# An adapter-plus-experts kernel: four buffers for x's parts, an own 98-row stack for the first tile's adapter product, a warm-up on a constant, folded parts ahead of bias sums

## What is computed

```python
y      = x @ W.T + b + 2.0 * (x @ lora_As[slot]) @ lora_Bs[slot]   # first layer, D = 512, R = 16
base   = y @ base_w.T + base_b                                     # second layer
hidden = y @ A.T                                                   # 128 x 64
probs  = softmax(y @ router_w.T)                                   # 128 x 16, two kept, divided by their sum
delta  = sum over experts e of  combine[e] * hidden @ B[e].T       # 1024 x 512 in all
out    = x + base + 0.5 * delta
```

## Time and profile before

| | us |
|---|---|
| median of three timed runs | 103.99 |
| lowest, highest | 103.49, 104.66 |
| the profiled execution: device time | 103.44 |
| the profiled execution: span of the profile | 101.6 |

### The profile page before, as it was taken

How to read it: one execution, slowest core, us unless ns; L and a number is a source line. 1 busy time by engine, 2 the same in 40 slices (tenths; PEclk the granted TensorE clock), 3 DMA queues, 4 the chain that set the end, 5 groups by cost and what they waited for, 6 DMA issues and landing times.

```text
span 101.6 us, 1806 instructions
## 1 busy us (share of the span) xinstructions
PE 97.4 (96%) x576; PEld 88.1 (87%) x576; DVE 65.1 (64%) x182; ACT 39.8 (39%) x97; POOL 18.7 (18%) x34
## 2 busy tenths in 40 slices
PE   5899999999999999999999999999999999999990
PEld 5799999999989999988988997899788788888990
DVE  2529999948567867959946735677368726656101
ACT  3404446885519726554435126120920604031000
POOL 5100003000397990070330061000000000000000
PEclk9999999999999999999999999999999999999999
DMA  2999789999854172592672280470065191940311
GB/s 42 321 318 377 225 182 372 340 424 422 230 96 68 26 216 58 168 267 68 182 254 59 79 231 1 117 205 6 14 165 165 20 266 46 239 170 0 110 52 52
DMA packets 8089, 16.91 MB, mean 166 GB/s; under 512 B 1475, under 2 KB 3907, under 8 KB 7952
## 3 DMA queue, kind: packets, MB, share of 16 engines
q1 hardware_dynamic: 7472, 16.40, 53.5%
q10 hardware_dynamic: 576, 0.39, 1.2%
q0 software_dynamic: 32, 0.00, 0.0%
HBM read 13.28 MB, written 2.16 MB: 152 GB/s over the span
## 4 chain that ended last, share of the span: by engine, by line
PE 71%; issue 11%; POOL 11%; DMA 3%; ACT 1%; DVE 0%; POOLq 0%
PE pair L771 69%; POOL x_lo L352 4%; POOL e_lo L370 4%; DMA w_raw_all<-w_cat 3%; POOL p_lo L364 2%; POOL p_hi L362 1%; PE pair L919 1%; PE pair L921 1%; ACT p_hi L418 1%; PE pair L939 1%; ACT w_hi_all L392 0%; DVE xn L765 0%; POOLq L361 0%
## 5 line engine op out<-in xcount | busy, mean ns | idle before, releaser
L771 PE MATMUL pair<-e_hi,w_hi_all 128*128 128x512 f32 (+1 forms) x72 | 27.2, 378 | 0.0
L771 PE MATMUL pair<-e_lo,w_hi_all 128*128 128x512 f32 (+1 forms) x72 | 26.7, 370 | 0.0
L771 PE MATMUL pair<-e_hi,w_lo_all 128*128 128x512 f32 (+1 forms) x72 | 26.6, 370 | 0.0
L771 PE MATMUL pair<-p_hi,x_hi 128*128 128x304 f32 x64 | 19.7, 308 | 0.2 <-POOL p_lo L364 0.2
L771 PE MATMUL pair<-p_lo,x_hi 128*128 128x304 f32 x64 | 19.4, 302 | 0.0
L771 PE MATMUL pair<-p_hi,x_lo 128*128 128x304 f32 x64 | 19.3, 302 | 0.0
L771 PEld LDWEIGHTS pair<-e_hi,w_lo_all 128*128 128x128 f32 x72 | 13.6, 188 | 2.6
L771 PEld LDWEIGHTS pair<-e_hi,w_hi_all 128*128 128x128 f32 x72 | 13.6, 188 | 2.4
L771 PEld LDWEIGHTS pair<-e_lo,w_hi_all 128*128 128x128 f32 x72 | 13.6, 189 | 1.8
L712 DVE TENSOR_TENSOR exp_raw_all<-w_raw_all 128x512 f32<-128x512 f32 x16 | 10.4, 689 | 7.5 <-DMA w_raw_all<-spill 7.5
L502 ACT ACTIVATE w_hi_all<-exp_raw_all 128x512 fp32r<-128x512 f32 x16 | 9.6, 627 | 13.8 <-DVE exp_raw_all L712 13.8
(11 more groups left out here) (107 smaller groups left out, 131.5 us busy)
## 6 DMA issues: line engine op xcount, KB each, us to landing
w_raw_all<-spill SPq DMA_DIRECT2D x16, 256.0 KB, 3.9
exp_raw_all<-experts SPq DMA_DIRECT2D x4, 512.0 KB, 8.7
xn<-x_n SPq DMA_DIRECT2D x4, 512.0 KB, 7.3
out<-xn SPq DMA_DIRECT2D x7, 256.0 KB, 4.0
w_raw_all<-w_cat SPq DMA_DIRECT2D x3, 552.0 KB, 6.8
xt_raw<-x_t SPq DMA_DIRECT2D x2, 512.0 KB, 6.3
xt_raw<-x_t SPq DMA_DIRECT2D x1, 1024.0 KB, 12.6
c_stack<-c_hi SPq DMA_DIRECT2D x7, 74.0 KB, 4.2
```

Source lines behind the costliest of these rows:

```text
L771: return nc.tensor.matmul(out_ap, lhs, rhs, start=first, stop=last)
```

## The change

1. **Warm-up.** It no longer reads `zeros` (F32R, set by DVE) but `nc.const_aps.tensor(0.0, (P, 2 * P), F32)`, a constant that the program's preamble sets, seen as 128x256; `WARM_UP` goes from 11 to 13; the wait for DVE is gone, and so is ACT's wait for the warm-up before `e_hi` is written.
2. **First tile.** `h_first` gets 2h rounded twice over (ACT, columns 0 to 15 and 64 to 79), the low part at column 32 (DVE), and ones at 96 and 97; its transpose, 98 rows, is copied once by ACT to `ht_first`; `c_first` (now `c_stack[:, 0]`) holds c high, c high again, c low and the bias rows at partitions 0, 32, 64 and 96, each copied there by ACT or DVE. The product is two matmuls. The bias rows of tiles 1 to 7 come by one DMA from it.
3. **x's parts** have four buffers (`XB`); those of tiles 2 and 3 lie in `w_hi` and `w_lo` of blocks 2 and 3, which are spent after the fold. ACT makes the high parts of tiles 2 and 3 right after the fold, POOL subtracts both before `lora_a_parts(2)`; for t >= 4 POOL does `lora_a_parts(t)` first.
4. **Bias sums.** `b1` and `b2` are issued behind the six tables; `b2` goes to row 0 of a zeroed 128x592 tensor, so the first bias sum is one instruction instead of two; the sums stand further back in DVE's order, behind the folded parts.
5. ACT splits the first half of W's first block in two pieces of 128 columns, and PE waits for each piece. `split_experts` stands elsewhere in ACT's order, and PE waits for POOL's expert parts only before the chunks that read them.

```diff
-WARM_UP = 11
+WARM_UP = 13
@@ tensors
-        b2_row = sb("b2_row", [1, D])
+        b2_rows = sb("b2_rows", [P, W2N])
-        zeros = e_hi[:, 0, 0:2 * P]
+        idle = nc.const_aps.tensor(0.0, (P, 2 * P), F32)
+        x_his, x_los = x_split(x_hi, w_hi), x_split(x_lo, w_lo)
@@ SP
-            sp.dma_start(b1_col[:, :], b1).then_inc(in_b, 16)
-            sp.dma_start(b2_row[:, :], b2).then_inc(in_b, 16)
             sp.dma_start(xt_raw[:, 0:2, :], x_t[:, 0:2, :]).then_inc(in_xt[0], 16)
...
+            sp.dma_start(b1_col[:, :], b1).then_inc(in_b, 16)
+            sp.wait_ge(first_set, 1)
+            sp.dma_start(b2_rows[0:1, SMALL:], b2).then_inc(in_b, 16)
@@ POOL
             x_lo_part(2)
+            x_lo_part(3)
             lora_a_parts(2)
             split_experts_lo(2)
-            x_lo_part(3)
             lora_a_parts(3)
             split_experts_lo(3)
             for t in range(4, NT):
+                lora_a_parts(t)
                 x_lo_part(t)
-                lora_a_parts(t)
@@ ACT
-            act.wait_ge(pe_warm, 1)
+            act.wait_ge(in_xt[1], 16)
+            x_hi_part(2)
+            x_hi_part(3)
             split_experts(0)
-            split_experts(1)
-            act.wait_ge(bias_step, KC + 1)
-            nc.scalar.activation(bp_hi[:, :], bias_part[:, :], ACT.Copy).then_inc(bph_done, 1)
             act.wait_ge(pe_c, 1)
             nc.scalar.activation(c_hi[:, :], w2_cols(ps_c), ACT.Copy).then_inc(ch_done, 1)
+            act.wait_ge(bias_step, KC)
+            nc.scalar.activation(bp_hi[:, :], bias_part[:, :], ACT.Copy).then_inc(bph_done, 1)
+            act.wait_ge(first_set, 2)
+            act.wait_ge(ch_done, 1)
+            nc.scalar.activation(c_first[0:R, :], c_hi[0:R, :], ACT.Copy).then_inc(first_high, 1)
@@ DVE
+            lora_first_lo()
+            dve.wait_ge(first_set, 2)
+            nc.vector.tensor_copy(c_first[F_AGAIN:F_AGAIN + R, :], c_hi[0:R, :]).then_inc(first_high, 1)
+            dve.wait_ge(cl_done, 1)
+            nc.vector.tensor_copy(c_first[F_LOW:F_LOW + R, :], c_lo[0:R, :]).then_inc(first_low, 1)
             split_experts_lo(0)
-            lora_first_lo()
             stack_bias()
@@ PE
-            pe.wait_ge(warm, 1)
             for _ in range(WARM_UP):
-                last = mm(ps_warm, zeros[:, 0:P], zeros, True, True)
-            last.then_inc(pe_warm, 1)
+                mm(ps_warm, idle[:, 0:P], idle, True, True)
...
@@ x_first
                 elif t == 1:
                     pe.wait_ge(cl_done, 1)
+                    pe.wait_ge(first_high, 2)
+                    pe.wait_ge(first_low, 1)
@@ lora_first_product
                 pe.wait_ge(ht_done, 1)
-                pe.wait_ge(ch_done, 1)
-                part(ht_first_hi[:, :], c_hi, False)
-                pe.wait_ge(cl_done, 1)
-                part(ht_first_hi[:, :], c_lo, False)
-                pe.wait_ge(ht_first_done, 1)
-                part(ht_first_lo[:, :], c_hi, False)
+                pe.wait_ge(first_high, 2)
+                pe.wait_ge(first_low, 1)
                 pe.wait_ge(bias_rows, 1)
-                part(ones[HR:HT, :], c_stack[HR:HT, 1, :], True).then_inc(pe_z, 1)
+                nc.tensor.matmul(ps_z[0][:, z_small[0]:BANK], ht_first[:, :], c_first[:, 0:border],
+                                 start=False, stop=True, skip_group_check=True)
+                nc.tensor.matmul(ps_z[0][:, BANK:BANK + W2N - border], ht_first[:, :], c_first[:, border:],
+                                 start=False, stop=True, skip_group_check=True).then_inc(pe_z, 1)
@@ lora_product
-                if t == 1:
-                    pe.wait_ge(bias_rows, 1)
-                else:
-                    pe.wait_ge(stacked_bias, 16)
+                pe.wait_ge(stacked_bias, 16)
```

More of the change, by code:

```diff
@@ L120, in adaln_ffn_kernel, with x_split @@
         rden = sb("rden", [P, 1])
+        def x_split(split, w_split):
+            return [split[:, b] for b in range(2)] + [
+                w_split[:, b, 0:D].rearrange("p (k n) -> p k n", k=KC) for b in range(2, XB)]
+        x_his, x_los = x_split(x_hi, w_hi), x_split(x_lo, w_lo)
         weight_rows = w_raw_all[:, 0:NB * GC * P].rearrange("p (a j n) -> p a j n", a=NB, j=GC)
@@ L391, in _ @@
             act.wait_ge(in_w_side[0], 16)
-            nc.scalar.activation(w_hi[:, 0, W_LEFT], w_raw[:, 0, W_LEFT], ACT.Copy).then_inc(wh_left, 1)
+            for cols in (slice(0, P), slice(P, 2 * P)):
+                nc.scalar.activation(w_hi[:, 0, cols], w_raw[:, 0, cols], ACT.Copy).then_inc(wh_left, 1)
             act.wait_ge(in_w_side[1], 16)
@@ L544, in _ @@
         def _(dve):
-            nc.vector.memset(zeros.bitcast(F32), 0.0).then_inc(warm, 1)
+            nc.vector.memset(b2_rows[:, :], 0.0).then_inc(first_set, 1)
+            nc.vector.memset(c_first.bitcast(F32), 0.0).then_inc(first_set, 1)
+            nc.vector.memset(h_first[:, :], 0.0).then_inc(first_set, 1)
             nc.vector.memset(ht[HR:HT, :, :].bitcast(F32), 1.0).then_inc(ht_set, 1)
             nc.vector.memset(routed[:, :, SMALL:T_H], 0.0).then_inc(ht_set, 1)
-            nc.vector.memset(low_row[HR:HT, :], -1.0).then_inc(low_row_set, 1)
-            dve.wait_ge(low_row_set, 1)
-            nc.vector.memset(low_row[HR:HR + 1, :], 0.0).then_inc(low_row_set, 1)
+            nc.vector.memset(low_row[F_BIAS:FT, :], -1.0).then_inc(first_set, 1)
+            dve.wait_ge(first_set, 4)
+            nc.vector.memset(h_first[:, F_BIAS:FT], 1.0).then_inc(first_set, 1)
+            nc.vector.memset(low_row[F_BIAS:F_BIAS + 1, :], 0.0).then_inc(first_set, 1)
             def first_block_hi(n, cols):
@@ L583, in x_lo_early @@
                 dve.wait_ge(xh_done, t + 1)
[L584 to L585 removed]
+                nc.vector.tensor_tensor(x_los[t], xt_raw[:, t, :].rearrange("p (k n) -> p k n", k=KC),
+                                        x_his[t].bitcast(F32),
                                         ALU.subtract).then_inc(xl_early, 1)
@@ L620, in _ @@
                                     ALU.subtract).then_inc(lbl_done, 1)
-            bias_part_of(0)
-            bias_part_of(1)
             folded_lo(0)
             folded_lo(1)
-            bias_part_of(2)
+            bias_part_of(1)
             folded_lo(2)
             folded_lo(3)
+            bias_part_of(2)
             bias_part_of(3)
+            dve.wait_ge(ch_done, 1)
+            nc.vector.tensor_tensor(c_lo[:, :], w2_cols(ps_c), c_hi[:, :].bitcast(F32),
+                                    ALU.subtract).then_inc(cl_done, 1)
             dve.wait_ge(bph_done, 1)
@@ L859, in x_side @@
                         pe.wait_ge(pl_done, KC)
-                    for n, (lhs, rhs) in enumerate(((x_hi, p_hi), (x_hi, p_lo), (x_lo, p_hi))):
-                        last = mm(ps_z[par][:, out_cols], lhs[:, par, k, :], rhs[:, k, cols],
+                    for n, (lhs, rhs) in enumerate(((x_h, p_hi), (x_h, p_lo), (x_l, p_hi))):
+                        last = mm(ps_z[par][:, out_cols], lhs[:, k, :], rhs[:, k, cols],
                                   k == 0 and n == 0, k == KC - 1 and n == 2)
```

130 lines of the change are left out of this document (61 added, 69 removed).

## The result

| | before | after |
|---|---|---|
| median of the timed runs, us | 103.72 (103.49 to 104.66) | 108.21 (107.29 to 108.60) |
| the profiled execution, us | 103.44 | 107.62 |
| its span, us | 101.6 | 105.7 |
| ratio after to before | | 1.040, 95% interval 1.033 to 1.047 |

Both medians are of five runs; the 103.99 further up is of the three that were there before the change.

The account below looks back on a forecast made before the run. TensorE's matmul stream was taken as the bound: its start, its length and a short tail. +4.26 - 1.0 - 0.25 = +3.0 us gave 106.4 on the profiled execution, 107.0 on the median; 106.7 was taken, range 104.8 to 109.0.

Parts of the forecast that it names:

- The warm-up, forecast at +4.26 us: Start of PE's stream: the fold begins 5.06 us later behind the longer warm-up, less 0.80 for faster first fold matmuls.
- everything behind it, forecast at -1.25: After the warm-up: 1.0 us saved at the first tile's product and 0.25 at the wait for POOL before `x_first(4)`.
- An F32 product is four passes: Warm-up: each F32 matmul takes four passes, 52 for 13 calls; with the clock rising within the warm-up, chance 0.80.
- The warm-up's end, 9.3 us: Warm-up on PE: 52 passes at 0.23 us until the clock rises at 5.5, then 0.12 each, end at 9.3.
- The slow matmuls come back: First six fold matmuls on PE: all run at the higher clock after the longer warm-up, giving back 0.80 us.
- The product, 1.0 us saved: First tile's product on PE: two matmuls replace eight and their holes, with PE about 0.1 us late for the bias rows.
- they are hidden with 0.4 to 0.5 us to spare: Before `x_first(1)`: ACT's and DVE's added copies ahead of the product end early enough that PE does not wait.
- POOL's chain, 0.25 saved: Before `x_first(4)`: POOL ends at 37.0 to 37.1, so PE's hole shrinks from 0.35 us to about 0.1.
- Bias sums: "Nothing": Later bias loads and DVE's sums: PE's margins for `lb_lo` and the folded parts suffice, so no time is lost.
- The one-pass rival: Warm-up: an F32 matmul costs one pass, the warm-up ends hidden at 3.9 us, total 102.6, 1.3% faster; chance 0.14.
- two passes for a call: Warm-up rival: 26 passes, end at 6.2 us, sum -0.1 us, total 103.9, no change; chance 0.04.
- the clock stay low to the end of the warm-up: Warm-up rival: four passes at the low clock throughout, end at 12.8 us, +7.3 us, total 111.3; chance 0.02.

Follow-up runs that it names:

- e1: The changed kernel with the warm-up's constant read as F32R instead of F32, still 13 matmuls: 104.73 us, ratio to before 1.006.
- e2: The kernel before with only the change's warm-up (13 F32 matmuls, no DVE memset, no ACT wait for the warm-up): 106.73 us, ratio to before 1.028.
- e4: The changed kernel with four F32 warm-up matmuls instead of 13: 104.75 us, ratio to before 1.008.
- e8: e1 with DVE's bias sums put back in the order of the kernel before: 103.61 us, ratio to before 0.997.
- e5: e1 with POOL waiting for DVE's last bias sum before x's low parts of tiles 2 and 3: 104.50 us, ratio to before 1.004.
- e7: e1 with the edits of both e5 and e6: 104.50 us, ratio to before 1.005.
- e6: e1 with DVE's subtraction of expert block 1 moved behind the routing of tile 1: 104.24 us, ratio to before 1.002.
- e9: e8 with expert block 1's subtraction given to POOL and ACT splitting expert block 2 before reading tile 1's h: 103.14 us, ratio to before 0.991.
- e10: e9 with tile 4's row copies issued behind the first routing trip instead of ahead of it: 103.50 us, ratio to before 0.991.

## Why the prediction was right, and where it was not

The forecast was slower, 106.7 us in a range of 104.8 to 109.0; measured 108.21, and 107.62 for the profiled execution against 106.4 forecast for it. The mechanism that carried it held. Two parts of the sum were off. The warm-up, forecast at +4.26 us, measured +3.35; everything behind it, forecast at -1.25, measured +0.75. The errors of -0.91 and +2.00 partly cancelled; that the number came out as near as it did is in part luck.

1. **An F32 product is four passes: right.** A call in the warm-up is two records, with starts 0.427 us apart at the lower clock and 0.218 at the higher; an F32R call of the same columns is one record, and the starts are 0.213 us apart at the lower clock (e1). So each of the two records costs two passes. e2 and e4 price it from both sides. The Trainium skill, "FP8 and Floating Point Precision", section "TensorE Precision Notes", gives four passes for true FP32; the trace agrees, with 2 x 0.427 us for a call against 0.213 for a pass.
2. **The warm-up's end, 9.3 us: too late by 1.0.** A pass cost 0.214 and 0.109, the columns alone, where I took 0.23 (an average with the first matmul's longer distance in it) and 0.12 (a stream that changes weights each time); and the clock rose 4.0 us after the first matmul instead of 4.7. The fold began at 8.27; the bound that I had worked out for columns only was 8.7. Net +3.35 instead of +4.26. The upper bound of this term, +5.4, is also 0.1 above what its own parts give (9.3 + 1.0 - 4.24 - 0.80 = 5.26).
3. **The slow matmuls come back: +0.80, measured 0.64.** Right in kind, and nearly in size: the first pair behind the warm-up took 0.46 only because the last warm-up record's 0.22 us fall into it. Items 2 and 3 share that overlap.
4. **The product, 1.0 us saved: the size of the work was right, the holes were not.** From the last matmul of `x_first(1)` to `x_other(1)` it takes 31.96 - 31.11 = 0.85 us instead of 1.51, which is 0.66 saved; the chain of the bias rows made a hole of 0.36 and not 0.1. The step "they are hidden with 0.4 to 0.5 us to spare" failed, with a hole of 0.28 us twice, as two bias sums took 3.11 us instead of 1.70 and `bp_hi`, which waits for them, stands ahead of h in ACT's order.
5. **POOL's chain, 0.25 saved: wrong.** The hole before `x_first(4)` went entirely, but one of 1.28 came ahead of `x_first(3)`, which the prediction had no wait for. It had taken ACT's, DVE's and POOL's durations from the kernel before as if they were the operations' own. Moving ACT's split of expert block 2 from 23.4 to 33.0 moved POOL's subtraction from 28.89 onto DVE's subtraction of block 1. The trace of before held a sign of it. The same DVE subtraction is there twice, once beside an idle POOL and once begun 0.44 us before POOL's own ended:

```profile
23.82 1.22 DVE L611 TENSOR_TENSOR e_lo<-exp_raw_all,e_hi 128x1024 fp32r<-128x1024 f32 x1
...
30.86 1.53 DVE L611 TENSOR_TENSOR e_lo<-exp_raw_all,e_hi 128x1024 fp32r<-128x1024 f32 x1
```

6. **Bias sums: "Nothing" was wrong**, 0.9 us by e1 against e8 (78.03 and 77.13 us from `x_first(0)` to the end); this is the same loss as that of the holes in item 4. The order of the sums looked free, as PE was far from needing them; that POOL's new low parts stood beside them was not looked at.

Steps 4 to 6 together: forecast -1.25 us, measured +0.75 (from `x_first(0)` to the end, 4.10 - 3.35). e5 and e7 show the cause for the sums and e8 what they are worth; e6 shows that the hole before `x_first(3)` goes with DVE's block 1, and in e9 and e10, where POOL has that block and ACT splits block 2 earlier, it goes without a new one before `x_first(4)`. Without these holes the forecast saving is largely there: e10 takes 97.84 - 21.35 = 76.49 us from `x_first(0)` to the end, 0.79 less than before, with a wait of 0.3 behind the trip through DRAM in it. A rule that would have told it is in the Trainium skill, "SBUF — State Buffer", section "Who interferes with whom": a DVE instruction with two inputs in SBUF contends with a GpSimd one that reads SBUF, and what they share is an exclusive lock. The traces agree, with 3.24 us for an operation of 1.23 that began 0.25 us behind one of 2.40.

The one-pass rival fell with e1 and e2; two passes for a call would have ended the warm-up near 6.2, and four calls (e4) would not have filled the time to 4.2. In neither kernel with 13 F32 calls did the clock stay low to the end of the warm-up.

## What to carry to other kernels

The type of an operand is part of a matmul's price, also where its value does not matter: a filler that must end by a given time is to be costed in passes, and its records counted in the trace. Before an operation is moved on VectorE or GpSimd, lay the two timelines side by side: a duration from the old trace holds only for the neighbours that it had there. And where two engines exclude each other, moving an operation can move the hole, as in e5 to e7. Putting the sums back where POOL idles and giving DVE's block to POOL took the holes away, from 0.6% above the kernel before to 0.9% below; 0.9 of these 1.5 points came with the sums (e8).

## What the runs showed that was not expected

- The moment at which TensorE's clock rises differs from one execution to the next. Read by the distance between matmuls, it is 3.4 us after the first matmul in e2, 4.0 in the changed kernel, 4.7 before and 6.2 in e1. The kernel's own start does not decide it: e1 and e6 to e10 have the same warm-up from 0.78 us on and begin the fold at 4.1 to 4.3, and in their traces the rise comes 6.2, 4.6, 4.3, 3.8, 5.5 and 5.0 us after the first matmul. A fold matmul has 0.247 us at the lower clock and 0.136 at the higher, so a microsecond of delay costs up to 0.45. An early rise does not bring all of that, as PE then meets the loads: in e8 it waits 0.4 us for ACT's next part of W, which itself waits for its DMA, and `x_first(0)` stands at 21.61 against 21.91 in e1, 0.3 earlier for 2.4 of clock. A difference between two single profiles is therefore best read from `x_first(0)` on.
- The granted clock of the warm-up's first part (0.78 to 4.70 us in the changed kernel) reads 1.00 in the profile, although the distances are those of the lower level (1.2 GHz); there the distances are to be read.
- VectorE's cast of one tensor, 16 rows of 592, is held up by GpSimd too (1.35 instead of 0.46 us in e7), and GpSimd's cast by VectorE's subtraction (1.24 instead of 0.24).
- Holes of 0.28 us between matmuls do not appear among PE's waits; only the distances between starts show them.
